# Maxima and exponentials of an attention pass at the same time, identity products ahead of all scores, the last four heads weighed together

## What is computed

```python
def step(carry, i):                      # 3 times, 16 heads of 8 features
    qcur, prev, attn, cw, temp, done = carry
    qp = qcur @ lq_w.T + lq_b            # kp, vp from k_full, v_full alike
    sq, sk = _ln(qp, lnc_w) * tscale, _ln(kp, lnd_w)
    scores = jnp.einsum('bhqd,bhkd->bhqk', sq, sk) * inv_sqrt_e
    scores = jnp.where(in_win[None, None, None, :], scores, -jnp.inf)
    probs = jax.nn.softmax(scores, axis=-1)
    out = jnp.einsum('bhqk,bhkd->bhqd', probs, vp)
    iter_out = jnp.where(in_win[None, None, :, None], out, 0.0)
    diff = jnp.mean(jnp.abs(iter_out - prev))   # decides the next window
    ...
```

## Time and profile before

| | |
|---|---|
| runs, us | 446.42, 459.40, 461.73 (median 459.40) |
| the profiled execution, us | 444.71 |
| its span from first to last instruction, us | 442.7 |
| mean granted PE clock | 0.822 of 2.4 GHz |
| busy | PE 309.9 us (70%), DVE 304.5 (69%), ACT 172.0 (39%), POOL 172.4 (39%) |

### The profile page before, as it was taken

How to read it: one execution, slowest core, us unless ns; L and a number is a source line. 1 busy time by engine, 2 the same in 40 slices (tenths; PEclk the granted TensorE clock), 3 DMA queues, 4 the chain that set the end, 5 groups by cost and what they waited for, 6 DMA issues and landing times.

```text
span 442.7 us, 7609 instructions
## 1 busy us (share of the span) xinstructions
PE 309.9 (70%) x2168; PEld 222.3 (50%) x2169; DVE 304.5 (69%) x859; ACT 172.0 (39%) x331; POOL 172.4 (39%) x281
## 2 busy tenths in 40 slices
PE   1896888788997889778788999216807200699960
PEld 1672216332353322478788999203807100689960
DVE  7598985995869994268755666566979760277850
ACT  1134553217601268053354555846024600345520
POOL 9572880740133344303575455300000087044560
PEclk9997559697999988969899999758775555699995
DMA  2599800000000000031224220694000022323310
GB/s 79 94 365 371 243 3 1 0 1 1 8 24 24 32 18 26 29 59 44 60 62 79 70 68 28 180 305 135 0 1 1 0 75 106 89 67 82 96 51 0
DMA packets 37805, 32.93 MB, mean 74 GB/s; under 512 B 10765, under 2 KB 28770, under 8 KB 37776
## 3 DMA queue, kind: packets, MB, share of 16 engines
q1 hardware_dynamic: 33792, 25.10, 20.3%
q0 software_dynamic: 3936, 7.49, 5.4%
q10 hardware_dynamic: 48, 0.00, 0.0%
HBM read 19.50 MB, written 13.98 MB: 76 GB/s over the span
## 4 chain that ended last, share of the span: by engine, by line
PE 36%; DVE 24%; DMA 18%; issue 7%; ACT 6%; POOL 4%; SPq 2%; DVEq 1%; POOLq 0%
DMA rows<-token_rows,posu 15%; PE ps L1247 12%; PE ps L1258 10%; POOL rows L585 4%; DVE mx L1775 3%; PE ps L1060 3%; PE ps L1055 2%; PE ps L1035 2%; DVE stats L1383 2%; PE ps L1231 2%; DMA xs<-rows 2%; SPq L293 1%; DVE wide L2017 1%; PE ps L1215 1%; DVE hb L1920 1%
## 5 line engine op out<-in xcount | busy, mean ns | idle before, releaser
L585 POOL DMA_INDIRECT rows<-token_rows,posu x48 | 50.5, 1053 | 142.3 <-DVE token_rows L1698 71.4
L1258 PE MATMUL ps<-w_out,hg 128*128 x496 | 66.1, 278 | 0.0
L1920 DVE TENSOR_TENSOR hb<-ps,b_in 128x512 f32<-128x512 f32 x62 | 42.7, 688 | 31.7 <-PE ps L1247 31.3
L1258 PEld LDWEIGHTS ps<-w_out,hg 128*128 128x128 f32 x496 | 61.0, 194 | 0.2
L597 POOL DMA_INDIRECT back<-ys,places x39 | 38.5, 988 | 48.5 <-DVE ys L1931 43.4
L866 ACT ACTIVATE hg<-hb 128x512 f32<-128x512 f32 x62 | 39.1, 630 | 37.5 <-DVE hb L1920 32.9
L1775 DVE TENSOR_REDUCE mx<-ps 128x2 f32<-128x512 f32 (+2 forms) x48 | 44.1, 947 | 2.3 <-PE ps L1035 1.7
L1247 PE MATMUL ps<-xsT,w_now 128*128 128x128 f32 x256 | 39.2, 302 | 5.9 <-DVE hb L1920 3.7
L1231 PE MATMUL ps<-ident,xs 128*128 128x128 f32 x62 | 18.1, 296 | 35.1 <-DMA xs<-rows 35.1
L1247 PEld LDWEIGHTS ps<-xsT,w_now 128*128 128x128 f32 x256 | 35.2, 213 | 7.5 <-issue 5.1
L765 ACT COPY qs<-ps 128x768 bf16<-128x768 bf16 (+1 forms) x21 | 15.3, 729 | 59.7 <-PE ps L1004 59.7
(11 more groups left out here) (390 smaller groups left out, 570.4 us busy)
## 6 DMA issues: line engine op xcount, KB each, us to landing
rows<-blank SPq DMA_DIRECT2D x20, 260.0 KB, 7.3
xs<-rows SPq DMA_DIRECT2D x62, 64.0 KB
w_in<-in_L_ffn_w_fc SPq DMA_DIRECT2D x1, 2048.0 KB, 15.1
w_in<-in_L_ffn_W SPq DMA_DIRECT2D x1, 2048.0 KB, 10.5
rest<-rows SPq DMA_DIRECT2D x23, 65.0 KB
token_rows<-in_L_attn_x SPq DMA_DIRECT2D x1, 832.0 KB, 8.1
wmod<-in_L_wmod SPq DMA_DIRECT2D x2, 384.0 KB, 4.3
rows<-token_rows,posu POOLq DMA_INDIRECT x48, 2.4
```

The source lines that it names most:

```text
L585: pool.indirect_dma_start(ROWS[l], bass.IndirectOffsetOnAxis(ap=posu[:, k, j:j + 1], axis=0), token_rows[:, j, 0:WIDTH[l]], None).then_inc ...
L1258: mm = pe.matmul(ps[:, 6 + c % 2, 0:D], hg[:, c % RING, n * P:(n + 1) * P], w_out[:, bass.ds(e * NB + n, 1), :], start=(n == 0), stop=(n = ...
L1920: v.tensor_tensor(hb[:, c % 2, :].rearrange("p (b t) -> p b t", b=NB), ps[:, c % RING if h_bank(l, t) is None else h_bank(l, t), :].rearra ...
```

## The change

- PSUM: the maxima's scores use banks 0 and 1, one bank for each part of at most 512 elements; a head's keys are cut so that nj query tiles fit in a bank (`KEY_PARTS`: one part in pass 0; 170 + 111 keys in pass 1; 170 + 139 in pass 2). The turned groups use banks 3, 4, 5, 6 (first four) and 2 (maxima), the exponents' scores banks 3-4 and 5-6 by turns, packed without gaps, so that a product is cut in two where it crosses a bank's border; the weighing uses bank 7 alone.
- PE turns all four groups ahead of the first score, and makes the scores of eight heads with a fill behind each of the first six. Then it makes a transposed score with a fill in front, and the plain score of the head eight further on, in one loop; weighing follows five heads behind.
- The last four heads are weighed tile by tile like the others, behind `turn_out(0)` and `turn_out(1)`.
- `count("far")` stands behind the loop of pass 1, and its columns are in bank 1.
- DVE reduces each part and takes the larger of two maxima in `stack_maxima`. ACT's copies 4 to 7 stand between its exponentials.
- The far scatter has two semaphores, so that two transfers may be in flight.

```diff
+KEY_PARTS = [[(a, min(a + 512 // -(-n // P), n)) for a in range(0, n, 512 // -(-n // P))] for n in WINDOWS]
+MAXIMA0 = [HEADS * sum(len(p) for p in KEY_PARTS[:it]) for it in range(3)]
...
+        COUNT_AT = {"far": ((1, 288), (1, 400)), "near": ((2, 0), (3, 256)), "all": ((3, 0), (4, 0))}
+        TURN_AT = (3, 4, 5, 6, 2, 2, 2, 2)
+        def exponents(h, n):
+            b = 3 + 2 * (h % 2)
+            return ps[:, b:b + 2, :].rearrange("p a n -> p (a n)")[:, 0:n]
...
                 for j in range(NA, NT):
-                    if j > NA:
-                        pool.wait_ge(sem("scattered_far"), 16 * sent)
-                    send_row("far", 0, k, j)
+                    if sent > 1:
+                        pool.wait_ge(sem(("scattered_far", "scattered_odd")[sent % 2]), 16 * (sent // 2))
+                    send_row("far", 0, k, j, odd=bool(sent % 2))
...
-                exps(0, 2)
+                stack_copy(it, 4)
+                exps(0, 3)
+                stack_copy(it, 5)
+                exps(3, 7)
+                take(0)
+                stack_copy(it, 6)
+                exps(7, 11)
+                take(1)
                 stack_copy(it, 7)
-                exps(2, 8)
-                take(0)
-                exps(8, 12)
-                take(1)
-                exps(12, 16)
+                exps(11, 15)
                 take(2)
+                exps(15, 16)
                 take(3)
...
+                def score(h):
+                    if h == 0:
+                        pe.wait_ge(sem("qs_first"), it + 1)
+                        pe.wait_ge(sem("ks_set" if it else "ks_act"), 2 * it - 1 if it else 4)
+                    elif h % 4 == 0:
+                        pe.wait_ge(sem("qs_act"), C0 + h // 4)
+                    if it and h == 4:
+                        pe.wait_ge(sem("ks_set"), 2 * it)
+                    parts = KEY_PARTS[it]
+                    for k, (lo, hi) in enumerate(parts):
+                        n = MAXIMA0[it] + len(parts) * h + k
+                        pe.wait_ge(sem("max_free"), n + 1)
                         for j in range(nj):
+                            mm = pe.matmul(ps[:, n % 2, j * (hi - lo):(j + 1) * (hi - lo)], half(qs, h)[:, j * P:(j + 1) * P],
+                                           half(ks, h)[:, lo:hi], start=True, stop=True)
                         mm.then_inc(sem("s_ready"), 1)
+                def turn_maxima(g):
+                    pe.wait_ge(sem("max_stack"), G0 + g + 1)
+                    pe.wait_ge(sem("qs_act"), C0 + 3 + g)
+                    turn(4 + g)
+                def score_t(h):
+                    if h >= 2:
+                        pe.wait_ge(sem("probs_ready"), H0 + h - 1)
+                    if h % 4 == 0:
+                        pe.wait_ge(sem("qs_act"), C0 + 4 + h // 4)
+                    fill(3 + 2 * (h % 2), 1)
+                    e = exponents(h, 1024)
+                    for j in range(nj):
+                        a = j * nw
+                        cuts = [a, a + nw] if a // 512 == (a + nw - 1) // 512 else [a, 512, a + nw]
+                        for lo, hi in zip(cuts, cuts[1:]):
+                            mm = pe.matmul(e[:, lo:hi], half(ks, h)[:, j * P:(j + 1) * P], half(qs, h)[:, lo - a:hi - a], start=True, stop=True)
+                    mm.then_inc(sem("st_ready"), 1)
...
                 turn(0)
+                turn(1)
                 if it:
                     pe.wait_ge(sem("asum"), it)
...
+                    pe.matmul(ps[:, 7, 0:1], ones[:], asum[:], start=True, stop=True).then_inc(sem("change"), 1)
+                else:
                     pe.wait_ge(sem("values"), 1)
+                turn(2)
+                turn(3)
+                fill(2, (1, 4, 10)[it])
+                for h in range(8):
+                    score(h)
+                    if h < 6:
+                        fill(2, 1)
+                    if h == 6:
+                        turn_maxima(0)
+                for h in range(HEADS):
+                    score_t(h)
+                    if h < 8:
+                        score(h + 8)
+                    if h % 4 == 2 and h < 11:
+                        turn_maxima(h // 4 + 1)
+                    g, k = divmod(h - 5, 4)
+                    if h >= 5 and k == 0:
+                        weigh_four(g, 0)
+                    elif h >= 5 and k == 1:
+                        weigh_four(g, 1)
+                        if nj == 3:
+                            weigh_four(g, 2)
                 if it == 1:
+                    count("far")
+                pe.wait_ge(sem("max_free"), MAXIMA0[it] + len(KEY_PARTS[it]) * HEADS + 2)
+                pe.wait_ge(sem("qs_act"), C0 + 7)
+                if it == 1:
+                    pe.wait_ge(sem("counts_read"), 1)
+                turn_out(0)
+                turn_out(1)
+                for jk in range(nj):
+                    weigh_four(3, jk)
                 turn_out(2)
                 turn_out(3).then_inc(sem("o_turned"), 1)
...
                 for h in range(HEADS):
+                    for k, (lo, hi) in enumerate(parts):
+                        n = MAXIMA0[it] + len(parts) * h + k
+                        v.wait_ge(sem("s_ready"), n + 1)
+                        v.tensor_reduce(mx[:, k, 0:nj, h:h + 1], ps[:, n % 2, 0:nj * (hi - lo)].rearrange("p (j n) -> p j n", j=nj), AX.X, ALU.max
+                                        ).then_inc(sem("max_free"), 1)
+                        if k == 0 and h % 4 == 0 and h:
+                            stack_maxima(h // 4 - 1)
                 stack_maxima(3)
```

More of the change, by code:

```diff
@@ L306, in build_adaln @@
         TURN_BANK = {"far": 3, "near": 2}
-        LOGIT_AT = {"far": (5, 0), "near": (3, 0)}
-        COUNT_AT = {"far": ((7, 0), (7, 256)), "near": ((2, 0), (3, 256)), "all": ((3, 0), (4, 0))}
+        LOGIT_AT = {"far": (7, 0), "near": (3, 0)}
+        COUNT_AT = {"far": ((1, 288), (1, 400)), "near": ((2, 0), (3, 256)), "all": ((3, 0), (4, 0))}
[3 more added lines that the diff above has]
+            return ps[:, b:b + 2, :].rearrange("p a n -> p (a n)")[:, 0:n]
         def tiles_before(l):
@@ L410, in wait_scattered @@
                     lo, hi, experts = GROUPS[g]
-                    sp.wait_ge(sem("scattered_" + g), 16 * (hi - lo) * experts)
+                    n = (hi - lo) * experts
+                    if g == "far":
+                        sp.wait_ge(sem("scattered_odd"), 16 * (n // 2))
+                        n -= n // 2
+                    sp.wait_ge(sem("scattered_" + g), 16 * n)
                 def wait_sent(tiles):
@@ L758, in _ @@
                 act.wait_ge(sem("kstackT"), g + 1)
[L759 removed]
+                act.copy(ks[:, 2 * g:2 * g + 2, :], turned(g, (0, 1, 2, 6)[g], NATT)).then_inc(sem("ks_act"), 1)
             def stack_copy(it, step):
@@ L764, in stack_copy @@
                 act.wait_ge(sem("stackT"), 8 * it + step + 1)
-                act.copy(qs[:, 2 * g:2 * g + 2, 0:n], turned(g, 6 + g % 2, n)).then_inc(sem("qs_act"), 1)
+                act.copy(qs[:, 2 * g:2 * g + 2, 0:n], turned(g, TURN_AT[step], n)).then_inc(sem("qs_act"), 1)
             def softmax_exp(it):
@@ L834, in _ @@
                     gap_exp("far")
-                for step in (4, 5, 6):
-                    stack_copy(it, step)
                 softmax_exp(it)
@@ L1019, in attend, with turn @@
                 H0, G0, C0 = HEADS * it, 4 * it, 7 * it
-                def turn(g):
-                    turn_group(g, 6 + g % 2, nj, "stackT")
+                def turn(step):
+                    turn_group(step % 4, TURN_AT[step], nj, "stackT")
                 def half(t, h):
                     return t[STK * (h % 2):STK * (h % 2) + STK, h // 2, :]
-                def scores(lo, hi):
-                    for h in range(lo, hi):
-                        b = h % 2
-                        pe.wait_ge(sem("max_free"), H0 + h + 1)
-                        if it and h >= 2:
-                            fill(3 * b, 1)
+                def score(h):
[10 more added lines that the diff above has]
+                        pe.wait_ge(sem("max_free"), n + 1)
@@ L1088, in attend @@
                 pe.wait_ge(sem("q_stack"), it + 1)
+                if it == 0:
+                    pe.wait_ge(sem("ks_act"), 4)
                 turn(0)
+                turn(1)
                 if it:
                     pe.wait_ge(sem("asum"), it)
-                    pe.matmul(ps[:, 3, 0:1], ones[:], asum[:], start=True, stop=True).then_inc(sem("change"), 1)
-                turn(1)
-                pe.wait_ge(sem("qs_first"), it + 1)
-                if it == 0:
-                    pe.wait_ge(sem("values"), 1)
-                    pe.wait_ge(sem("ks_act"), 4)
-                else:
-                    fill(4, (1, 4, 10)[it])
-                    pe.wait_ge(sem("ks_set"), 2 * it - 1)
@@ L1117, in attend @@
-                scores(12, 16)
-                turn_maxima(2, 4)
-                scores_t(0, 2)
```

(25 more changed lines are left out.)

78 lines of the change are left out of this document (22 added, 56 removed).

## The result

The changed kernel takes 470.7 us (median of four runs, 467.8 to 477.1), the kernel before 455.3 (446.4 to 461.7) in the same session. The ratio is 1.047, 95% interval 1.026 to 1.067: slower, outside the range forecast. Ratios here compare only runs within 1.5% of the fastest of each kernel; medians are over all of them, so the two can differ.

What follows compares the result with a forecast made beforehand. Far-scatter chain and pass 2 were taken to end together, so the passes' ends count. Terms −1.0 + 1.0 + 2.5 + 2.2 − 2.7, less 0.5, gave +1.5 us, ratio 1.003: 454 us, range 438 to 465.

Steps and rivals of the forecast that it cites:

- the one for pass 1: Pass 1: PE's products up to the count sum to 32.8 us; next_queries starts at 43.8, not 41.3, +2.5.
- the one for pass 2: Pass 2: PE's products sum to 40.0 us at full clock against 42.7, −2.7; no gain if PE falls again.
- a step of 1.16, not 1.35: Pass 1's mixed part: fill, transposed score and plain score take 1.35 us on PE, which becomes the bound.
- the late count: Pass 1: DVE reads counts behind the loop, then plans 10.6 us; next_queries at 43.8, DVE never waiting for o_turned.
- the gap before pass 2: Before pass 2: PE idles nearly 5 us and goes cold, slowing 24 transposes and ten fills: +2.2, between 0 and +3.5.
- scatter steps of 1.3 us: Far scatter: two transfers in flight cut a step from 2.72 to 1.3 us, 36 us in all, worth 0.5 us.
- 54.5 forecast: Pass 0: last maximum at 54.5, DVE free 14.4 us later, at 68.9 against 70.90; −1.0 taken.
- rival 2: All passes: dense work keeps the clock up and pieces overlap; pass 0 gives −2, −7 us in all; chance 0.12.
- The start of pass 1: Ahead of pass 1's first maximum: two more transposed groups before the first score, 6.0 us against 4.95, +1.0.
- Rival 3: Pass 0: PE stays cold, mixed step 1.45 us, +5.6; one more cold stretch in pass 2; +11, 464 us; chance 0.17.
- DVE's 14.5 us: Pass 2: DVE's other work behind the maxima starts some 23.5 us in and ends at 38, just covered.
- The handover's −0.5: Pass 2 to experts(0): with the scatter off the chain, experts start about 0.5 us earlier.

Runs made afterwards that it cites:

- 3: Changed kernel with one far-scatter transfer in flight, as before the change: 482.6 us (467.8 to 484.6).
- 6: Changed kernel with scores multiplied over all 128 rows, both heads of a pair at once, which alters the output: 446.1 us, ratio 0.987.
- 9: Keys in two copies with zeros in the other 64 rows, values unchanged: changed kernel 449.9 us, with count at head 12 444.4, kernel before 443.5.
- 5: Changed kernel with two fills for one in passes 1 and 2: 460.1 us, ratio 1.018.
- padded changed kernel: Changed kernel with zero-padded keys, scores over all 128 rows, values unchanged: 449.9 us, ratio 0.999.
- variant with the early count: Changed kernel with zero-padded keys and the far count at head 12 of pass 1: 444.4 us, ratio 0.986.
- 4: Changed kernel with the far count behind head 12 of pass 1 instead of head 15: 477.0 us, ratio 1.044.
- 1: Changed kernel with plain scores of passes 1 and 2 cut by query tile, three parts a head, instead of by keys: 493.8 us.
- before padded: Kernel before the change with zero-padded keys alone: 443.5 us, ratio 0.982.
- 8: Kernel before the change with added fills, among pass 0's scores and ahead of every transposed score: 472.0 us, ratio 1.032.
- 7: Kernel before the change with two far-scatter transfers in flight and nothing else: 457.6 us, ratio 1.008.
- the fastest one: Kernel before the change with zero-padded keys and two far-scatter transfers in flight: 440.4 us, ratio 0.973.

## Why the prediction was wrong

**The step that failed** is the clock in the terms for pass 1 and pass 2. Both sums were made at full clock: the one for pass 1 without saying so, the one for pass 2 with the words that the pass gains nothing "if PE falls again". It fell in both, for 27 us in pass 1 (85.4 to 112.4) and 30 in pass 2 (157.7 to 187.7): 52.3 against 43.8 and 52.8 against 40.0, 21.3 us in all. Some 6 of these are the waits that end by "remote" (without them pass 2 took 47.0 us in 3, still cold), the rest is the clock. I took a PE without idle time for a warm one, though two rows of my own, 104.6 to 111 and 162 to 168.3, showed a busy PE at 0.50 and 0.55. That the 64 rows of the scores let the clock fall in passes 1 and 2 is shown by 6 and 9, which keep the number of products, their columns and their order; 5 shows the same from the other side, with more full-row products among them. They don't make it fall each time: pass 0 has products over 64 rows too and ran at either level. Why one run of it falls and another doesn't stays open.

The Trainium skill (TensorE: Matmul & The Clock Gate, "What's actually happening") has the clock follow from how busy PE has been, and I cited it for the fills. The trace agrees for a PE that waits (143.34, granted 0.50 to 0.51 behind 3.18 us of idle) and disagrees for 92.0 to 112.4, 20.40 us busy of 20.40 at 0.50; the measurement decides.

**The full-clock arithmetic was nearly right, its comparison was not.** The padded changed kernel of 9 is the one that I had costed: a step of 1.16, not 1.35; the counts read 30.8 us after the first maximum, not 33.2; pass 1 41.4, not 43.8; pass 2 43.5 with its clock at 0.88, and 40.8 at 0.96 in its variant with the early count, for 40.0. But 42.7 us, from which I subtracted 40.0, held a cold stretch. At full clock the kernel before takes 39.6. The gain of 2.7 was a warm sum against a partly cold measurement.

**Right** were: the late count (next_queries 10.6 us behind the counts, DVE not waiting for o_turned in pass 1), its place on the path (4, and 3.7 us in 9); the gap before pass 2, +2.2 as forecast, out of an idle PE (3.18 us, not nearly 5) and ten fills of 3.95; scatter steps of 1.3 us, worth nothing by themselves. In pass 0 the maxima ended at 53.85 (54.5 forecast) and the sum was read at 68.18, −2.7, near rival 2's −2; that is luck in part, since the same code took 41.5 us in the profiles of 1 and 4. The start of pass 1 was +0.4 instead of +1.0. Rival 3 had the mechanism, a PE that is cold in the mixed steps, but I had let it act in pass 0 and "one more cold stretch", and priced it at 11.

**Missed**: how late the maxima of pass 2 end. I let DVE's 14.5 us start 23.5 us after the first maximum; they started 28.8 us after it in the padded changed kernel and 26.1 in its variant with the early count. In the changed kernel, with the last maxima reduced at 187.89 to 189.08, the sum is read behind them at 203.93, just as PE ends. The handover's −0.5 did not come either: what follows pass 2's sum took 262.2 us instead of 259.7. No run settles why; in the other profiles in which the scatter isn't last it takes 260.7 to 266.5.

**Open**: the waits that end by "remote". In the changed kernel's passes they are two of DVE's, 3.07 and 3.09 us in pass 2. The second ends at 168.53, and SyncE's first read behind the whole scatter is issued at 168.55:
```profile
168.55 1.76 SPq L391 DMA_DIRECT2D xs<-rows  x4
```
From the start of pass 1 to the end of pass 2, DVE has such waits of over 2 us in seven profiles, all of kernels with two transfers in flight; the four kernels with one (before, before padded, 3 and 8) have none, and five with two (1, 6, 7, the padded changed kernel, the fastest one) have none either. Later on kernels with one in flight have them too (3.32 us until 221.76 in the padded kernel before, 3.05 until 254.47 in 3), when their far scatter is long over. So two in flight isn't enough for them, and that it is needed isn't shown. What is waited for, no run here shows.

## What to carry to other kernels

Read the granted clock of the busy stretches, not only of the idle ones: where PE is busy at the lower level and its products take half the rows, padding the operand with zeros is an edit to try before any reordering; here it was worth 1.8% by the ratio, 15.5 us at the median. Profile more than one execution where the clock can fall either way, and make both sides of a sum at the same clock. Before two phases are overlapped, list what the engine of the first phase has queued behind it; here DVE's other work had been hidden under the second phase, and the overlap uncovered it.

## What the runs showed of the hardware

- From 92.0 to 112.4 PE was busy for 20.40 of 20.40 us and granted 0.50 with scores over 64 rows and single fills; it was granted 1.00 with the same kinds of products over 128 rows, half of them zeros (19.27 of 20.40 us busy).
- A product over 128 rows takes as long as one over 64: at full clock 0.53 us for 843 columns, as three products over 64 rows or as four over 128 (94.65 above).
- The same code of pass 0 took 28.5 us at 0.98 to 1.00 in three profiles (the changed kernel, 3, 5) and 41.4 to 41.5 at 0.50 in two (1, 4); in the six profiles with padding pass 0 was 24.9 to 27.2 us at 0.81 to 1.00.
